# Stencil rows in a four-stage model kernel: eight matrix products per batch written as four, one row carried by a copy and a small DMA, and a new order of the work

## What is computed

```python
x = L0(x)   # whole-tile norm, scale/shift, silu, @W_in, norm, silu, @W_out, + x
x = L1(x)   # attention, 16 heads, bias fside[b,h,q,k], mask; then a 256-1024-256 feed-forward
x = L2(x)   # one step of a stencil on the 256 x 256 grid
x = L3(x)   # causal attention, 16 heads; a 256-1024-256 feed-forward; gate
```

```python
df = -(grad(A0*f, rows) + grad(A1*f, cols)) \
     + 0.5*(grad2(B0*f, rows) + grad2(B1*f, cols) + 2*grad(grad(B2*f, cols), rows))
x  = maximum(f + dt[b]*df, 0)
```

## Time and profile before

| | |
|---|---|
| median of 3 runs | 2919.82 us (2919.42 to 2924.5) |
| the profiled execution | 2922.63 us, its span 2921.3 us |
| PE busy | 2679.7 us, 92% of the span |
| ACT, DVE, POOL busy | 2352.2, 2240.3, 1683.2 us |
| PE of 600 to 2600 us | 1933.69 us busy of 2000, granted clock 1.00 |

### The profile page before, as it was taken

One profiled execution on the slowest core, in us unless ns is written; L12 is line 12 of the kernel. 1 busy time (PEld: TensorE's weight loads), 2 busy tenths in 40 slices (PEclk: granted clock), 3 DMA queues, 4 the chain that ended last, 5 costly groups with the idle time before them and its releaser, 6 DMA issues.

```text
span 2921.3 us, 61436 instructions
## 1 busy us (share of the span) xinstructions
PE 2679.7 (92%) x19916; PEld 2223.0 (76%) x19916; DVE 2240.3 (77%) x7850; ACT 2352.2 (81%) x5286; POOL 1683.2 (58%) x1736
## 2 busy tenths in 40 slices
PE   4678999999999999999999999999999999999866
PEld 3456788888888888888888888888888888887654
DVE  4556888888888888888888888888888888887533
ACT  1456888988888889888888888888888888888654
POOL 1456666565666665656666656566666666666211
PEclk8789999999999999999999999999999999999988
DMA  5223333333333333333333333333333333333110
GB/s 204 92 92 97 109 103 92 108 100 97 101 109 113 98 98 105 102 97 100 109 112 97 101 100 107 97 100 109 112 95 103 97 109 97 100 106 101 27 29 19
DMA packets 175088, 287.86 MB, mean 99 GB/s; under 512 B 44784, under 2 KB 98032, under 8 KB 174384
## 3 DMA queue, kind: packets, MB, share of 16 engines
q1 hardware_dynamic: 174768, 283.94, 32.8%
HBM read 174.64 MB, written 8.45 MB: 63 GB/s over the span
## 4 chain that ended last, share of the span: by engine, by line
PE 75%; ACT 13%; DVE 5%; issue 4%; POOL 1%; SPq 1%; DMA 0%; DVEq 0%; ACTq 0%; POOLq 0%
PE bank L960 17%; PE bank L967 16%; PE bank L988 10%; PE bank L937 10%; PE bank L945 7%; PE bank L980 4%; PE bank L1075 4%; ACT PB L799 3%; PE bank L952 2%; PE bank L1004 2%; PE bank L1005 2%; ACT L906 1%; ACT BB L816 1%; ACT AA L816 1%; DVE PO L620 1%
## 5 line engine op out<-in xcount | busy, mean ns | idle before, releaser
L799 ACT ACTIVATE PB<-PB,mx 128x256 f32<-128x256 f32 (+1 forms) x2048 | 840.2, 475 | 136.0 <-DVE mx L612 135.0
L620 DVE TENSOR_TENSOR PO<-bank,PH 128x384 f16<-128x384 f32 (+1 forms) x1024 | 634.8, 620 | 245.5 <-ACT PH L805 235.8
L805 ACT ACTIVATE PH<-bank 128x384 f16<-128x384 f32 (+1 forms) x1024 | 546.3, 534 | 140.3 <-PE bank L988 135.7
L386 POOL TENSOR_TENSOR BT<-BT,MN 128x1024 f32<-128x1024 f32 x256 | 557.5, 2188 | 129.5 <-DMA BT<-in_bias 129.3
L988 PE MATMUL bank<-ident,PB 128*128 128x128 f32 x3584 | 587.8, 281 | 26.4 <-DVE PO L620 13.5
L980 PE MATMUL bank<-Ks,Qs 96*128 96x512 f32 (+1 forms) x1024 | 530.4, 519 | 34.6 <-DMA Ks<-KU 21.8
L988 PEld LDWEIGHTS bank<-ident,PB 128*128 128x128 f32 x3584 | 422.9, 143 | 107.5 <-ACT PB L799 53.7
L612 DVE CUSTOM_DVE_ANT_0 PB<-bank,BT 128x256 f32<-128x256 f32 x1024 | 388.2, 417 | 42.7 <-PE bank L980 17.7
L612 DVE CUSTOM_DVE_ANT_0 PB<-bank,caus 128x128 f32<-128x128 f32 (+1 forms) x1024 | 321.7, 351 | 125.9 <-PE bank L988 71.1
L1004 PEld LDWEIGHTS bank<-VP,PH 128*128 128x128 f16 x3584 | 207.9, 97 | 98.5 <-issue 58.5
L960 PE MATMUL bank<-TN,Wf 128*128 128x256 f32 x1024 | 261.2, 399 | 20.3 <-ACT BB L816 16.1
(11 more groups left out here) (204 smaller groups left out, 5212.3 us busy)
## 6 DMA issues: line engine op xcount, KB each, us to landing
BT<-in_bias SPq DMA_DIRECT2D x256, 512.0 KB, 3.7
Qs<-QH SPq DMA_DIRECT2D x512, 64.0 KB, 2.4
Ks<-KH SPq DMA_DIRECT2D x1024, 32.0 KB, 2.0
Qs<-QU SPq DMA_DIRECT2D x256, 64.0 KB, 2.3
Ks<-KU SPq DMA_DIRECT2D x512, 32.0 KB, 2.0
XT<-in_xT SPq DMA_DIRECT2D x32, 256.0 KB, 2.9
X<-in_x SPq DMA_DIRECT2D x32, 256.0 KB, 2.9
AB<-ada_rows SPq DMA_DIRECT2D x32, 256.0 KB, 3.3
```

Source lines behind the costliest of these rows:

```text
L386: G.op.tensor_tensor(v2(BT[k % 3]), v2(BT[k % 3]), MN[:, :].unsqueeze(1).broadcast_to([128, 2, 512]), ALU.add).then_inc(g_bt, 1)
L620: V.op.tensor_tensor(PO[i][:, 0:w], bP[h][:, 0:w], PH[i][:, 0:w], ALU.subtract).then_inc(v_low, 1)
L799: S.op.activation(o, o, ACT.Exp, scale=-1.0, bias=mx[u.layer][:, c:c + 1]).then_inc(a_exp, 1)
L805: S.op.activation(PH[i][:, 0:w], bP[h][:, 0:w], ACT.Copy).then_inc(a_high, 1)
```

## The change

The two products of the shifted matrices are written as one with the row above and one with the row below: with `low = (B0+A0)/2*X - w` and `up = (B0-A0)/2*X + w` (`w` is half the column difference; `cH` is 0.25 instead of 0.5 of B2), row i of the result is a row of one moved down plus a row of the other moved up, and the middle term of `G2` goes into `cB`. Inside a half this is one 128 x 128 block for each of `up` and `low`: four products. The row that crosses from one half to the other is put in the free place at the edge: `up`'s by a copy on VectorE (one partition, 256 elements), `low`'s by a DMA of one row of 256 elements (`s_row`, on SP). The blocks are made once by `row_moves()`, and `coefficients()` has more steps. Nearly every number of `P` is new (pieces of L3 count from their own beginning):

```diff
 P = {
-    "score0": -1, "score1": 2, "bias0": 2, "bias1": 3, "exp0": 4, "exp1": 5, "flip0": 6, "flip1": 8,
-    "high0": 7, "high1": 9, "low0": 8, "low1": 10, "pv0": 11, "pv1": 11, "pvn": 13,
-    "ld_bt": -3, "mask_add": -3, "stack": -2,
-    "ld_x": -93, "ld_xn": -39, "ld_ab": -27, "ld_mask": -36, "mask": -18,
-    "n1_stats": -76, "n1_ones": -73, "n1_sum": -72, "n1_center": -71, "n1_rstd": -70, "n1_scale": -63,
-    "n1_tanh": -62, "n1_gate": -62, "win": -56, "win_out": -50,
-    "n2_stats": -46, "n2_ones": -43, "n2_sum": -40, "n2_center": -40, "n2_rstd": -40, "n2_scale": -39,
-    "n2_tanh": -37, "n2_gate": -37, "xb": -39, "wout": -36, "x1": -34, "x1_rstd": -31, "x1_norm": -31,
-    "ada": -27, "t1": -27, "t1_out": -26, "x1_bo": -8, "q1": -23, "q1_out": -18, "q1_lo": -15,
-    "k1": -18, "k1_out": -16, "k1_lo": -14, "v1": -16, "v1_out": -10, "v1_hi": -8, "v1_sub": -7, "v1_mid": 2,
-    "v1_lo": 6,
-    "c1": 42, "c1_out": 43, "o1": 45, "m1": 46, "m1_rstd": 47, "m1_norm": 48, "m1_b": 62, "t2": 48, "t2_out": 49,
-    "w1": 52, "w1_out": 54, "w1_gelu": 62, "w2": 63, "f1": 67,
-    "s_pm": 71, "s_r": 71, "s_rp": 72, "s_re": 78, "s_ha": 71, "s_w": 78, "s_p2": 78, "s_mm": 81, "s_f": 95,
-    "coef": -16, "coefs": -27,
-    "m3": -53, "m3_rstd": -47, "m3_norm": -40, "t3": -39, "t3_out": -38, "y3": -39, "q3": -34, "q3_out": -30,
-    "q3_lo": -26, "k3": -26, "k3_out": -22, "k3_lo": -9, "v3": -22, "v3_out": -22, "v3_hi": -16, "v3_sub": -2,
-    "v3_mid": 1, "v3_lo": 9, "c3": 43, "c3_out": 46, "o3": 46, "m4": 46, "m4_rstd": 49, "m4_norm": 50, "m4_b": 75,
-    "t4": 50, "t4_out": 51, "w3": 52, "w3_out": 54, "w3_gelu": 62, "w4": 63, "out": 79, "st_out": 89,
+    "score0": -1, "score1": 1, "bias0": 1, "bias1": 3, "exp0": 3, "exp1": 5, "flip0": 7, "flip1": 7,
+    "high0": 8, "high1": 8, "low0": 10, "low1": 10, "pv0": 13, "pv1": 13, "pvn": 15,
+    "ld_bt": -9, "mask_add": -4, "stack": -8,
+    "ld_x": -121, "ld_xn": -44, "ld_ab": -24, "ld_mask": -32, "mask": -30,
+    "n1_stats": -91, "n1_ones": -67, "n1_sum": -67, "n1_center": -64, "n1_rstd": -65, "n1_scale": -63,
+    "n1_tanh": -61, "n1_gate": -61, "win": -50, "win_out": -49,
+    "n2_stats": -40, "n2_ones": -39, "n2_sum": -36, "n2_center": -36, "n2_rstd": -35, "n2_scale": -34,
+    "n2_tanh": -33, "n2_gate": -33, "xb": -30, "wout": -30, "x1": -29, "x1_rstd": -28, "x1_norm": -25,
+    "ada": -21, "t1": -20, "t1_out": -20, "x1_bo": -16, "q1": -18, "q1_out": -17, "q1_lo": -15,
+    "k1": -16, "k1_out": -13, "k1_lo": -13, "v1": -12, "v1_out": -7, "v1_hi": -2, "v1_sub": 3, "v1_mid": 4,
+    "v1_lo": 8,
+    "c1": 45, "c1_out": 45, "o1": 47, "m1": 49, "m1_rstd": 49, "m1_norm": 52, "m1_b": 57, "t2": 53, "t2_out": 55,
+    "w1": 58, "w1_out": 59, "w1_gelu": 65, "w2": 67, "f1": 71,
+    "s_pm": 72, "s_b": 74, "s_r": 72, "s_rp": 74, "s_re": 78, "s_ha": 75, "s_w": 78, "s_ab": 88, "s_row": 93,
+    "s_mm": 96, "s_f": 104,
+    "coef": -24, "coefs": -17,
+    "m3": -40, "m3_rstd": -39, "m3_norm": -34, "t3": -33, "t3_out": -32, "y3": 20, "q3": -31, "q3_out": -29,
+    "q3_lo": -13, "k3": -25, "k3_out": -21, "k3_lo": -11, "v3": -20, "v3_out": -20, "v3_hi": -18, "v3_sub": 7,
+    "v3_mid": 10, "v3_lo": 15, "c3": 45, "c3_out": 45, "o3": 46, "m4": 47, "m4_rstd": 50, "m4_norm": 51, "m4_b": 61,
+    "t4": 52, "t4_out": 52, "w3": 54, "w3_out": 55, "w3_gelu": 66, "w4": 68, "out": 78, "st_out": 80,
 }
```

The code, by engine: SP, GpSimd, VectorE (`stencil`), TensorE, and VectorE once near the start (the semaphore `v_s` counts 17 instead of 15 in a batch, all waits on it follow):

```diff
+                for b in at(t, "s_row"):
+                    S.wait_ge(v_s, 17 * b + 14)
+                    S.op.dma_start(AA[3][127:128, 256:512], AA[3][127:128, 0:256]).then_inc(d_row, 16)
...
+                for b in at(t, "s_b"):
+                    G.op.tensor_tensor(AA[3][:, :], X[b % 5][:, :], cL[:, :], ALU.mult).then_inc(g_s, 1)
                 for b in at(t, "s_ha"):
                     G.op.tensor_tensor(AA[0][:, :], x[:, :], cH[:, :], ALU.mult).then_inc(g_s, 1)
-                    G.op.tensor_tensor(AA[1][:, :], x[:, :], cA0[:, :], ALU.mult).then_inc(g_s, 1)
-                for b in at(t, "s_p2"):
-                    G.wait_ge(v_s, 15 * b + 8)
-                    G.op.tensor_tensor(AA[0][:, :], x[:, :], cB0[:, :], ALU.mult).then_inc(g_s, 1)
+                    G.op.tensor_tensor(AA[1][:, :], x[:, :], cU[:, :], ALU.mult).then_inc(g_s, 1)
...
                     ends(eg, X[b % 5], w1, n + 8)
-                    V.op.tensor_tensor(w1[:, :], w1[:, :], m[:, :], ALU.subtract).then_inc(v_s, 1)
+                for b in at(t, "s_ab"):
+                    V.wait_ge(v_s, n + 12)
+                    V.wait_ge(g_s, 5 * b + 5)
+                    V.op.tensor_tensor(m[:, :], m[:, :], w1[:, :], ALU.add).then_inc(v_s, 1)
+                    V.op.tensor_tensor(low[:, :], low[:, :], w1[:, :], ALU.subtract).then_inc(v_s, 1)
+                    V.wait_ge(v_s, n + 13)
+                    V.op.tensor_copy(m[0:1, 0:256], m[0:1, 256:512]).then_inc(v_s, 1)
...
                 for b in at(t, "s_mm"):
-                    T.wait_ge(d_G, 16)
-                    T.wait_ge(v_s, 15 * b + 13)
-                    T.wait_ge(g_s, 5 * b + 5)
-                    for q in range(2):
-                        n = 0
-                        for a, w in ((0, AA[2]), (1, AA[0])):
-                            for k in range(2):
-                                c = a * 512 + k * 256 + q * 128
-                                last = T.op.matmul(half(bM, q), Gm[:, c:c + 128], half(w, k), start=False, stop=(n == 3),
-                                                   skip_group_check=True)
+                    T.wait_ge(v_mv, 10)
+                    T.wait_ge(v_s, 17 * b + 15)
+                    T.wait_ge(d_row, 16 * (b + 1))
+                    for q, up, low in ((0, 1, 0), (1, 2, 3)):
+                        for n, (k, w) in enumerate(((up, AA[1]), (low, AA[3]))):
+                            last = T.op.matmul(half(bM, q), Gm[:, 128 * k:128 * k + 128], half(w, q), start=False,
+                                               stop=(n == 1), skip_group_check=True)
...
+            def row_moves():
+                blk = [Gm[:, 128 * i:128 * i + 128] for i in range(8)]
+                V.wait_ge(d_G, 16)
+                for i in (4, 7):
+                    V.op.tensor_tensor(blk[i], blk[i], ident[:, :], ALU.add).then_inc(v_cf, 1)
+                for n, (up, lo, d2) in enumerate(((1, 0, 4), (2, 3, 7))):
+                    V.wait_ge(v_cf, 26 + n)
+                    V.op.tensor_tensor(blk[up], blk[d2], blk[lo], ALU.add).then_inc(v_mv, 1)
+                    V.wait_ge(v_mv, 5 * n + 1)
+                    V.op.tensor_tensor(blk[lo], blk[d2], blk[lo], ALU.subtract).then_inc(v_mv, 1)
...
```

More of the change, by code:

```diff
@@ L134, in build @@
         gT, bT = sb("gT", [128, 512]), sb("bT", [128, 512])
-        cA0, cB0, cP, cM, cB, cH = (sb(n, [128, 512]) for n in ("cA0", "cB0", "cP", "cM", "cB", "cH"))
+        cU, cL, cP, cM, cB, cH = (sb(n, [128, 512]) for n in ("cU", "cL", "cP", "cM", "cB", "cH"))
+        fold = sb("fold", [128, 2])
         er, eg = sb("er", [128, 16]), sb("eg", [128, 16])
@@ L317, in loads @@
                         S.op.dma_start(Gm[:, :], A["G"]).then_inc(d_G, 16)
-                        for o, a in ((cA0, A["A"][0]), (cB0, A["B"][0]), (sA1, A["A"][1]), (sB1, A["B"][1]), (sB2, A["B"][2])):
+                        for o, a in ((cU, A["A"][0]), (cL, A["B"][0]), (sA1, A["A"][1]), (sB1, A["B"][1]), (sB2, A["B"][2])):
                             S.op.dma_start(o[:, :], a).then_inc(d_sten, 16)
@@ L422, in gpsimd @@
                     x = X[b % 5]
-                    G.wait_ge(v_cf, 14)
+                    G.wait_ge(v_cf, 25)
                     G.wait_ge(v_f1, b + 1)
@@ new lines, in coefficients @@
+                    V.op.tensor_scalar(e4(eg[:, :], i), e4(eg[:, :], i), 0.5, None, ALU.mult).then_inc(v_cf, 1)
+                for q, e in ((0, 0), (1, 127)):
+                    V.op.tensor_scalar(fold[:, q:q + 1], ident[:, e:e + 1], 0.5, 1.0, ALU.mult, ALU.subtract).then_inc(v_cf, 1)
+                for q in range(2):
+                    V.wait_ge(v_cf, 16 + q)
+                    V.op.scalar_tensor_tensor(out=half(cB, q), in0=half(cL, q), scalar=fold[:, q:q + 1], in1=half(b1, q),
+                                              op0=ALU.mult, op1=ALU.subtract).then_inc(v_cf, 1)
+                    V.op.scalar_tensor_tensor(out=er[:, 8 * q:8 * q + 8:7], in0=half(cL, q)[:, 0:256:255], scalar=fold[:, q:q + 1],
+                                              in1=er[:, 8 * q:8 * q + 8:7], op0=ALU.mult, op1=ALU.add).then_inc(v_cf, 1)
@@ new lines, in coefficients @@
+                V.wait_ge(v_cf, 15)
+                V.op.tensor_tensor(b2[:, :], cL[:, :], cU[:, :], ALU.subtract).then_inc(v_cf, 1)
+                V.wait_ge(v_cf, 22)
+                V.op.tensor_tensor(cL[:, :], cL[:, :], cU[:, :], ALU.add).then_inc(v_cf, 1)
+                V.wait_ge(v_cf, 23)
+                V.op.tensor_scalar(cU[:, :], b2[:, :], 0.5, None, ALU.mult).then_inc(v_cf, 1)
```

(20 more changed lines are left out.)

35 lines of the change are left out of this document (17 added, 18 removed).

## The result

| | before | after |
|---|---|---|
| median of the runs | 2919.62 us (4 runs) | 2892.64 us (4 runs, 2877.28 to 2896.08) |
| ratio of the means | | 0.9895, 95% interval 0.9856 to 0.9934 |
| profiled execution, its span | 2921.3 us span | 2896.08 us, span 2894.8 us |
| granted clock over the span | 0.973 | 0.953 |

What follows compares the result with a forecast made beforehand. PE's own work was taken to set the time in the middle (96.7% busy). 2922.6 - 56 (products) + 6 (waits) - 4 (start) - 3 (end) = 2865.6 us profiled, 2863 against the median, given as 2861; range 2822 to 2902.

Steps and rivals of the forecast that it cites:

- The products: Stencil on PE: eight products become four, saving 1.75 us in each of 32 batches, 56 us (52 to 59).
- plain half: Stencil products: half of the 3.27 us between starts, 1.64 us a batch, beside a difference of 1.73.
- The period: Time per batch: 82.5 us before, from 31 distances of `s_f`; 81.0 us expected after.
- The places: PE's waits at the new places: -0.99 at `o3`, +1.5 at `t4`, -0.3 at `w1`/`w3`; +0.2 us a batch, 6 us.
- The wait of 1.5 us at `t4`: PE before `t4`: chain of 4.8 us against 3.2 us of cover, a new wait of 1.6, taken as 1.5.
- VectorE: Two operations and a copy replace one: +0.1 to +1.8 us a batch, hidden by 14 us free; costed at nothing.
- The row's DMA: Row moved on SP before the products: 7 us against some 9 us of PE work, hidden with some 2 to spare.
- slower: Rival: PE stands at `s_mm` because the row has not landed; 2956 us, chance 0.08.
- Start and end: First batch some -4 us (shorter wait, slow products); last two batches -3 us (0 to -6), with `w4` at 68.
- More: Rival: the wait at `t4` does not come, 1.5 us less in 28 batches; 2819 us, chance 0.17.
- Less: Rival: ACT falls behind after the gelu, 0.9 us a batch lost; 2886 us, chance 0.22.
- Nothing: Rival: PE's freed time turns whole into waits, another engine being the bound; 2920 us, chance 0.05.

Runs made afterwards that it cites:

- e7: e6 with four more products a batch that add zero; 2875.69 us, ratio 0.9843.
- e6: Changed kernel with edge multiplications reading one input from PSUM (other edge values) and both crossing rows by DMA, no VectorE copy; 2823.06 us, ratio 0.9669.
- e4: Kernel before (eight products, no copy, no DMA) at the new places, s_p2 at tick 88; 2912.66 us, ratio 0.9971.
- e5: Changed kernel with the edge multiplications reading one input from PSUM instead of X (other edge values); 2829.05 us, ratio 0.9687.
- e3: New stencil (four products, copy, DMA) at the places of the kernel before, s_row 79, s_mm 84; 3170.36 us, ratio 1.0865.
- e8: e3 with s_row at 91, s_mm at 94 and s_f at 98; 3068.9 us, ratio 1.051.
- e9: Changed kernel, whole computation kept, with the four edge multiplications on GpSimd and both crossing rows by DMA; 2831.18 us, ratio 0.9694.
- e1: Changed kernel with the edge work s_re and s_w at tick 81 instead of 78; 2873.2 us, ratio 0.9842.
- e12: e9 with the column difference and its two reductions at tick 80 instead of 78; 2854.84 us, ratio 0.9767.

## Why the prediction was off where it was

The time fell inside the range, 31.6 us above the forecast, of which 2 us are between the sum, 2863, and the 2861 that was given without a reason. Against the runs, by terms:

- **The products** (forecast -56 us, ends 52 and 59): 52.6 us by e7 and e6, the "plain half" of 1.64 a batch, at the low end. In an undisturbed batch of the middle it is 1.7, as the difference of starts (1.73) had it. The term is right.
- **The period.** 82.5 us a batch was worked out over all 31 distances of `s_f`, and those at the start and end are shorter. In the middle it is 83.57. The forecast of 81.0 after was met by nothing: 80.4 in a clean batch, 82.79 in the mean.
- **The places** (forecast +6 us): the step "sum: -0.99 + 1.5 - 0.3 = +0.2 us a batch" failed. By e4 they give -1.5 us a batch at full clock. `o3`'s wait went as said. The wait of 1.5 us at `t4` is there, in part under another name. PE in the clean batch from 1460.86 us:

```profile
1508.01 0.50 PE L1032 MATMUL bank<-Ks,Qs 96*128 96x512 f32 x1 [1.00 <-DVE mx L658]
...
1510.29 0.66 PE L1004 MATMUL bank<-ident,TC 128*128 128x128 f32 x4 [0.35 <-ACT TC L862]
```

  The score before `t4` takes 1.00 us of it, `t4` itself 0.35. PE's idle time per batch is the same, 2.75 before (83.57 - 80.82) and 2.63 after (80.59 - 77.96), and what shrank is its busy time, by 1.2 us more than the products. By the starts of the records in one batch of each kernel, idle time taken off, the 112 `flip` products take about 12.8 us instead of 13.7, and the others are within some tenths. That is a reading; no run isolated it. My sum was of labelled waits, and such a gain carries no label.
- **VectorE** (forecast: "I cost it at nothing", "the forecast would stay while VectorE's free time holds it"): this is the step that failed, by 69.6 us (after less e6). 63.6 of them go with the edge multiplications (after less e5), and in these are the meetings of the difference, six in after's 27 batches and none in e5, and some of the copy's, eleven against four; the other 6.0 are the rest of the copy's (e5 less e6). The forecast priced a meeting for the two new operations only, and these never met. It was the old ones that met the mask addition, and their own numbers in `P`, 78, had not changed: what moved was `mask_add`, from -3 to -4, and the pieces around them. And 17% of idle time on VectorE doesn't hide 2 us just where a score waits for its bias: PE pays it at once, and then in clock. The Trainium skill, "SBUF — State Buffer", section "SBUF: two separate sides", was weighed in the prediction and set aside; its rule is what the rows show, here to 0.1 us. The Trainium skill, same page, section "Who interferes with whom", says that an operation of VectorE with at most one input in SBUF doesn't contend with GpSimd unless it runs in a mode that uses both ports, which a copy can: e5 (multiplications of at most 0.17 us inside the mask addition) and the copy's 2.2 us agree.
- **The row's DMA** (forecast: hidden with some 2 us to spare): hidden, with no wait of PE; it landed in 1.7 us, not 2.0. At the old places the rival *slower* was real, by SP's queue: at least 101 us (e3 less e8), since the time without the wait holds new meetings.
- **Start and end** (forecast -4 and -3): +4.9 and -11.0. In e6 and e9 the start takes 280.4 and 278.3 us to the fourth x1, 280.3 before; so the 4.9 is again the meetings, and without them the start's gain is 0 to 2 us. The end's gain is 11 to 16 us in after, e6 and e9, more than the one wait in the earlier trace rows was worth; I did not take it apart. The slices in which PE is busy for over 90% begin at about 290 us and not at 150, as the section on the time before has it.
- **The rivals.** *More* (2819) is what the kernel does with the meetings taken out (e6, 2823), by its own reason only in part. *Less* (2886) came nearest to the time, but not by the gelu: there is no wait of PE there among those above. *Nothing* didn't occur.

Put together from before to after, in medians: places and everything else without meetings -43.7 (before to e7), products -52.6 (e7 to e6), meetings +69.6 (e6 to after, good to some 10 us). So it is partly luck that the time lay inside the range: the places with start and end, forecast at -1 us in all, gave some 44, and the meetings, forecast at nothing, took some 70.

## What to carry to other kernels

Before moving work of VectorE, or of GpSimd beside it, list all of VectorE's operations in the moved stretch that have two inputs in SBUF (and its copies there), with the 8-element ones among them, and lay GpSimd's longest operation over each: in these runs the smallest waited as long as the largest. Idle share says nothing of it; ask whose wait ends right behind the operation, and if it is TensorE's, reckon with the clock as well as with the wait. And after every move look for new meetings: e1, e8 and e12 each took one wait or meeting away and brought another. What can't be moved can be freed of the port: one input in PSUM, or the small work given to GpSimd itself, as in e9, which kept the whole result and gave 3.1% where the change alone gave 1.0%.
